# Cross-attention of a decoder layer: weights in chunks, early loads from a second queue, stores moved, products spaced

## What is computed

```python
q = x @ Wq.T ; k_raw = context @ Wk.T ; v_raw = context @ Wv.T
# 32 heads of 16; k and v are read as interleaved pairs of one 1024-wide row
q = rmsnorm(q) ; k = rmsnorm(k)            # over the 16 elements of a head
attn = softmax(q k^T * 16**-0.5)
x = layernorm(x + attn @ v)
```

## Time and profile before

| what | us |
|---|---|
| median of the two timed runs | 2721.75 |
| the profiled execution's own time | 2720.43 |
| its span, first to last instruction | 2718.7 |
| busy: PE | 2443.4 |
| busy: ACT | 1358.8 |
| busy: DVE | 1338.2 |
| busy: POOL | 901.9 |

### The profile page before, as it was taken

One profiled execution on the slowest core, in us unless ns is written; L12 is line 12 of the kernel. 1 busy time (PEld: TensorE's weight loads), 2 busy tenths in 40 slices (PEclk: granted clock), 3 DMA queues, 4 the chain that ended last, 5 costly groups with the idle time before them and its releaser, 6 DMA issues. The chain is left out here.

```text
span 2718.7 us, 38977 instructions
## 1 busy us (share of the span) xinstructions
PE 2443.4 (90%) x15376; PEld 1565.7 (58%) x15376; DVE 1338.2 (49%) x2097; ACT 1358.8 (50%) x1722; POOL 901.9 (33%) x593
## 2 busy tenths in 40 slices
PE   7996799989999999999995899997589999999997
PEld 5875444434444444444224555564478788888776
DVE  5575434334343434343105555554365566666675
ACT  4221357656766777677993443433322255555221
POOL 1234554644465445555003433331022011120320
PEclk9997899999999999999997999999799999999999
DMA  4002665385638554765435100000344266665341
GB/s 170 16 1 80 204 157 137 95 214 146 171 72 227 149 152 102 194 166 140 115 68 200 49 1 16 2 17 1 134 139 131 86 220 211 228 222 176 113 127 51
DMA packets 208437, 333.01 MB, mean 122 GB/s; under 512 B 70976, under 2 KB 125504, under 8 KB 208064
## 3 DMA queue, kind: packets, MB, share of 16 engines
q1 hardware_dynamic: 193200, 262.49, 34.1%
q0 software_dynamic: 15056, 68.03, 7.5%
HBM read 243.10 MB, written 99.42 MB: 126 GB/s over the span
## 5 line engine op out<-in xcount | busy, mean ns | idle before, releaser
L861 ACT ACTIVATE c_prob<-c_psum 128x1024 f32<-128x1024 f32 x832 | 786.3, 1031 | 317.1 <-PE c_psum L1057 308.6
L809 POOL TENSOR_TENSOR c_rr<-c_ms,c_half 128x32 f32<-128x32 f32 (+1 forms) x72 | 372.8, 5179 | 450.0 <-DVE c_ms L878 449.9
L1066 PE MATMUL c_psum<-c_prob,c_vq 128*17 128x512 f32 x3328 | 416.4, 600 | 6.1 <-DVE c_oT L981 6.0
L1057 PE MATMUL c_psum<-c_qq,c_kq 64*128 64x512 f32 x1664 | 292.4, 439 | 35.6 <-ACT c_prob L861 17.7
L1057 PEld LDWEIGHTS c_psum<-c_qq,c_kq 64*128 64x128 f32 x1664 | 137.4, 185 | 196.4 <-ACT c_prob L861 109.7
L918 DVE COPY c_raw<-c_psum 128x256 f32<-128x256 f32 x91 | 38.7, 425 | 364.8 <-PE c_psum L120 364.8
L120 PE MATMUL c_psum<-c_w_hi,c_c_hi 128*128 128x512 f32 x416 | 179.0, 430 | 15.1 <-POOL c_c_lo L802 11.5
L1418 DVE TENSOR_REDUCE s_topx<-s_psum 128x4 f32<-128x2048 f32 (+1 forms) x64 | 95.5, 1492 | 183.3 <-PE s_psum L1508 183.3
L120 PE MATMUL m_psum<-m_t_hi,m_up_hi 128*128 128x256 f32 (+1 forms) x552 | 159.4, 289 | 23.9 <-DVE m_t_lo L2168 23.9
L1941 ACT ACTIVATE m_a_hi<-m_work 128x256 fp32r<-128x256 f32 (+2 forms) x113 | 56.7, 501 | 244.4 <-DVE m_work L2017 238.2
L1066 PEld LDWEIGHTS c_psum<-c_prob,c_vq 128*17 128x17 f32 x3328 | 68.7, 96 | 185.2 <-issue 160.9
(11 more groups left out here) (283 smaller groups left out, 5018.3 us busy)
## 6 DMA issues: line engine op xcount, KB each, us to landing
c_kq<-kd SPq DMA_DIRECT2D x248, 208.0 KB, 6.1
c_c_raw<-in_ctxT SPq DMA_DIRECT2D x104, 256.0 KB, 3.6
c_qq<-qd SPq DMA_DIRECT2D x64, 256.0 KB, 3.2
vd<-c_vt SPq DMA_DIRECT2D x104, 136.0 KB, 2.0
c_vq<-vd SPq DMA_DIRECT2D x31, 442.0 KB, 9.4
kd<-c_t_hi SPq DMA_DIRECT2D x48, 256.0 KB, 2.2
kd<-c_t_lo SPq DMA_DIRECT2D x48, 256.0 KB, 2.6
m_hs<-slots SPq DMA_DIRECT2D x23, 512.0 KB, 7.3
```

Of the source, the lines that this page charges most:

```text
L809: pool.tensor_tensor(rr[:, unit % RB, 0:n], ms[:, unit % RB, 0:n], half[:, 0:n], ALU.pow).then_inc(s_r, 1)
L861: act.activation(prob[:, t % PB, 2 * (u % 2):2 * (u % 2) + 2, :], score_banks[u % 3], ACT.Exp, scale=XD ** -0.5).then_inc(s_ex, 1)
L1057: mm = pe.matmul(score_banks[u % 3][:, s, :], kq[rows, q % 2, u % 2, kt * P:(kt + 1) * P], qq[rows, q % 2, u % 2, :], start=True, stop=True)
L1066: mm = pe.matmul(o_bank[32 * j:32 * j + VW, :], vq[:, q % 2, kt, j, :], prob[:, t % PB, j, :], start=kt == 0, stop=kt == CT - 1)
```

## The change

It is confined to cross-attention:

- Wq is loaded in four chunks with a semaphore each; ACT splits each chunk, DVE makes the low parts after X 0 and X 1 in place of before them, and PE's first query product waits chunk by chunk. The two halves of the key/value weights have a semaphore each.
- KV 13 and KV 14 move from the blocks into the prologue, behind KV 12 (`EARLY = CT + 2`). ACT, not POOL, splits their tiles.
- In the prologue ACT issues the loads of context tiles 4 to 18 itself; from KV 15 on SP loads tile i + 4 ahead of the store of values i.
- Of batch entry 0's queries only chunk 0 is stored in the prologue; chunks 1 to 3 are stored after the load of quad 1. The other entries' stores stay. A quad's load waits for the store of its own chunk alone (`s_qst[c]`).
- The planner wants a block without a heavy piece between a KV and the heavy piece before it, except behind a Q; the due times of a half begin earlier (13 or 10 blocks before its edge in place of 8), even halves end one block earlier, and a heavy piece goes into a block with two value groups after four blocks in place of three.

```diff
+    EARLY = CT + 2
...
-                kv(6), kv(7), t(5), kv(8), kv(9), t(6), kv(10), kv(11), t(7), kv(12)]
+                kv(6), kv(7), t(5), kv(8), kv(9), t(6), kv(10), kv(11), t(7), kv(12), kv(13), kv(14)]
...
+        heavy = [x for x in heavy if x[1:] not in self.of]
...
-            begin, end = (0 if h == 1 else edge(h - 1) - 8), edge(h) - (11 if h % 2 else 13)
+            begin, end = (0 if h == 1 else edge(h - 1) - (13 if h % 2 else 10)), edge(h) - (11 if h % 2 else 14)
...
-        turns = [8, 9, 10]
+        turns = [8, 9, 10, 11]
...
+        unit_done, last_heavy, after_q = {8: -9, 9: -2, 10: -1, 11: -1}, -1, False
...
-                return placed(self.kind_of(self.job_of(kind, i) - 2), 2)
+                return placed(self.kind_of(self.job_of(kind, i) - 2), 2) and last_heavy <= k - 2 + after_q
...
-            elif heavy_ready() and (len(ready) < 2 or k >= due[heavy[0]] + 3):
-                got = heavy.pop(0)
+            elif heavy_ready() and (len(ready) < 2 or k >= due[heavy[0]] + 4):
+                got, last_heavy = heavy.pop(0), k
+                after_q = got[0] == "Q"
...
+        def load_ctx(eng, n):
+            if n >= CB:
+                eng.wait_ge(s_clo, n - CB + 1)
+            eng.dma_start(c_raw[:, n % CB], d["ctxT"][n // CT // 2, n % CT].rearrange("p (k t) -> p k t", k=KC)).then_inc(s_c[n % CB], 16)
...
+                    if piece.i >= line.EARLY and piece.i + CB < 2 * B * CT:
+                        load_ctx(sp, piece.i + CB)
                     store_values(piece)
-                    if piece.i + CB < 2 * B * CT:
-                        load_ctx(piece.i + CB)
-                    if h % 2 == 0 and 4 <= lt < 4 + KC:
+                    if h % 2 == 0 and 4 <= lt < 4 + (KC if h else 1):
                         store_queries(h // 2, lt - 4)
...
-                if g == 0 and first == 0:
-                    sp.wait_ge(s_qst, 16 * 4 * KC * (b + 1))
                 if first == 0:
+                    sp.wait_ge(s_qst[c], 16 * 4 * (b + 1))
...
-            sp.dma_start(wq_raw[:], d["WqT"].rearrange("(k p) n -> p k n", p=P)).then_inc(s_wq, 16)
+            for k in range(KC):
+                sp.dma_start(wq_raw[:, k], d["WqT"][k * P:(k + 1) * P]).then_inc(s_wq[k], 16)
             for i in range(2):
-                load_ctx(i)
+                load_ctx(sp, i)
...
                         load_quad(1, 0, CT, s_quad[1])
+                        for c in range(1, KC):
+                            store_queries(0, c)
...
-                    if job < B * line.JPB and line.kind_of(job)[0] == "KV" and line.kind_of(job)[1] >= CT:
+                    if job < B * line.JPB and line.kind_of(job)[0] == "KV" and line.kind_of(job)[1] >= line.EARLY:
...
-            act.wait_ge(s_wq, 16)
-            act.activation(wq_hi[:], wq_raw[:], ACT.Copy).then_inc(s_whi, 1)
+            for k in range(KC):
+                act.wait_ge(s_wq[k], 16)
+                act.activation(wq_hi[:, k], wq_raw[:, k], ACT.Copy).then_inc(s_wqhi, 1)
...
-            for n in range(CT):
-                if n + 2 < CT:
+            for n in range(line.EARLY):
+                if n + 2 < line.EARLY:
                     high_part(n + 2)
+                load_ctx(act, n + CB)
...
+                if (piece.kind, piece.i) == ("X", 1):
+                    for k in range(KC):
+                        dve.wait_ge(s_wqhi, k + 1)
+                        dve.tensor_tensor(wq_lo[:, k], wq_raw[:, k], wq_hi[:, k], ALU.subtract).then_inc(s_wqlo, 1)
...
+                    if (piece.kind, i) == ("Q", 0):
+                        for k in range(KC):
+                            pe.wait_ge(s_wqlo, k + 1)
+                            mm = product3(pe, dst[:], lambda _: lhs[0](k), lambda _: lhs[1](k), lambda _: rhs[0](k), lambda _: rhs[1](k), 1, first=k == 0, last=k == KC - 1)
+                    else:
+                        mm = product3(pe, dst[:], *lhs, *rhs, KC)
...
```

More of the change, by code:

```diff
@@ L559, in softmax @@
         put_at.update({(p.kind, p.i): -9 for p in self.prologue})
-        unit_done = {8: -9, 9: -2, 10: -1}
+        unit_done, last_heavy, after_q = {8: -9, 9: -2, 10: -1, 11: -1}, -1, False
         done, line_up = 0, self.QT + self.KU
@@ L678, in cross_attention @@
         s_apart = m.sem("apart")
-        s_const, s_w, s_wq, s_whi, s_wlo = m.sem("const", "w", "wq", "whi", "wlo")
+        s_const, s_w, s_wq = m.sem("const"), m.sem("w0", "w1"), m.sem(*[f"wq{k}" for k in range(KC)])
+        s_wqhi, s_wqlo, s_whi, s_wlo = m.sem("wqhi", "wqlo", "whi", "wlo")
         s_c, s_chi, s_clo = m.sem(*[f"c{i}" for i in range(CB)]), m.sem("chi"), m.sem("clo")
@@ L683, in cross_attention @@
         s_ms, s_r, s_kn, s_own = m.sem("ms", "r", "kn", "own")
-        s_qst = m.sem("qst")
+        s_qst = m.sem(*[f"qst{c}" for c in range(KC)])
         s_kst, s_vst, s_quad = m.sem("kst0", "kst1"), m.sem("vst0", "vst1", "vst2"), m.sem("quad0", "quad1")
@@ L717, in store_queries @@
                     for r in range(2):
-                        sp.dma_start(qd[b, c, :, a, :, r, :], part[:, c].bitcast(F32)).then_inc(s_qst, 16)
+                        sp.dma_start(qd[b, c, :, a, :, r, :], part[:, c].bitcast(F32)).then_inc(s_qst[c], 16)
             def store(piece):
@@ L754, in load_quad @@
                 sp.dma_start(vq[:, buf, first:last].rearrange("p l h e -> p l (h e)"), vd[b, :, first:last, g * HG * VW:(g + 1) * HG * VW]).then_inc(s_done, 16)
-            sp.dma_start(wq_raw[:], d["WqT"].rearrange("(k p) n -> p k n", p=P)).then_inc(s_wq, 16)
+            for k in range(KC):
+                sp.dma_start(wq_raw[:, k], d["WqT"][k * P:(k + 1) * P]).then_inc(s_wq[k], 16)
             for i in range(2):
-                load_ctx(i)
+                load_ctx(sp, i)
             for s in range(2):
-                sp.dma_start(w_raw[:, :, s * H:(s + 1) * H], d["WkvT"][:, s * H:(s + 1) * H].rearrange("(k p) n -> p k n", p=P)).then_inc(s_w, 16)
+                sp.dma_start(w_raw[:, :, s * H:(s + 1) * H], d["WkvT"][:, s * H:(s + 1) * H].rearrange("(k p) n -> p k n", p=P)).then_inc(s_w[s], 16)
             for i in range(2, CB):
-                load_ctx(i)
+                load_ctx(sp, i)
             pieces = [(line.FIRST[i], line.FIRST[i + 1]) for i in range(3)]
@@ L768, in first_quad @@
                         if i == 0:
-                            sp.wait_ge(s_wlo, 3)
+                            sp.wait_ge(s_wqlo, KC)
+                            sp.wait_ge(s_wlo, 2)
                         load_quad(0, a, z, s_first[i])
@@ L826, in _ @@
         def _(act):
-            act.wait_ge(s_wq, 16)
-            act.activation(wq_hi[:], wq_raw[:], ACT.Copy).then_inc(s_whi, 1)
+            for k in range(KC):
+                act.wait_ge(s_wq[k], 16)
+                act.activation(wq_hi[:, k], wq_raw[:, k], ACT.Copy).then_inc(s_wqhi, 1)
             def high_weights(s):
-                act.wait_ge(s_w, 32)
+                act.wait_ge(s_w[s], 16)
                 act.activation(w_hi[:, :, s * H:(s + 1) * H], w_raw[:, :, s * H:(s + 1) * H], ACT.Copy).then_inc(s_whi, 1)
@@ L849, in _ @@
                 act.wait_ge(s_put, piece.index + 1)
-                if n % 2 == 0 and unit >= RB:
+                if n % CT % 2 == 0 and unit >= RB:
                     act.wait_ge(s_put, turned_before(unit))
-                act.activation(raw[:, unit % RB, n % 2 * HD:n % 2 * HD + HD], src[:, 0:HD], ACT.Copy).then_inc(s_k, 1)
+                act.activation(raw[:, unit % RB, n % CT % 2 * HD:n % CT % 2 * HD + HD], src[:, 0:HD], ACT.Copy).then_inc(s_k, 1)
                 if v_stored(n):
@@ L891, in low_weights @@
             def low_weights(s):
-                dve.wait_ge(s_whi, s + 2)
+                dve.wait_ge(s_whi, s + 1)
                 dve.tensor_tensor(w_lo[:, :, s * H:(s + 1) * H], w_raw[:, :, s * H:(s + 1) * H], w_hi[:, :, s * H:(s + 1) * H], ALU.subtract).then_inc(s_wlo, 1)
@@ L921, in take @@
                     dve.tensor_copy(vt[:, v_buf(i), :, 0:XD], heads(src[:, HD:H])).then_inc(s_v, 1)
-                if piece.kind == "KV" and early and i + 2 < CT:
+                if piece.kind == "KV" and early and i + 2 < line.EARLY:
                     split_low(i + 2)
@@ L928, in take @@
                         if b and j == 0:
-                            dve.wait_ge(s_qst, 16 * 4 * KC * b)
+                            for c in range(KC):
+                                dve.wait_ge(s_qst[c], 16 * 4 * b)
                         hi, lo = (t[:, :, j * P:(j + 1) * P] for t in (q_hi, q_lo))
@@ L961, in layer_norm @@
                 return LayerNorm(dve, X, lambda t: b * TT + t, (stats, mv, ve, rstd), Count(dve, s_norm, b * LayerNorm.STEPS), s_ve, s_rstd, s_apart, b)
-            dve.wait_ge(s_whi, 1)
-            dve.tensor_tensor(wq_lo[:], wq_raw[:], wq_hi[:], ALU.subtract).then_inc(s_wlo, 1)
             dve.wait_ge(s_const, 4)
@@ L1018, in put @@
                     if piece.kind == "Q":
-                        pe.wait_ge(s_wlo, 1)
```

(5 more changed lines are left out.)

4 lines of the change are left out of this document (removed).

## The result

The changed kernel took 2690.15 us (two runs, 2688.51 to 2691.78) against 2721.75: ratio 0.9884, 95% interval [0.9841, 0.9926]. Run again beside the experiments it took 2687.03 us (ratio 0.9895, [0.9873, 0.9918]). The forecast was 2680, its range 2660 to 2698. The span fell by 31.9 us (2718.7 to 2686.8) where the sum had 41.2.

What follows compares the result with a forecast made beforehand. Prologue bound by what PE waits for, blocks by PE itself. Terms: prologue -20.3, two KV -4.0, spacing -19.5, quad 6 -11.4, stall +14, sum -41.2 us; against 2721.75 this gives 2680 us, range 2660 to 2698.

Steps and rivals of the forecast that it cites:

- Weight, -6.1: Prologue start: chunked loading and splitting let PE's first query product end at 236.6 against 242.7, 6.1 us less.
- Context tiles on ACT: Prologue: tiles issued by ACT remove 15.4 us of PE waits and 4.5 us of half clock behind them.
- rival B: Prologue: tiles late from ACT too, engines being the same 16, and chunks gain only 2.7 us; 2696 us, chance 15%.
- KV 13 and 14 in the prologue, +5.7: Prologue: the two moved products add 12 matmuls each at full clock, 5.7 us together.
- two blocks lose 4.0 us: Blocks that lose KV 13 and KV 14 fall from 4.88 to 2.86 us each, -4.0 us.
- The stall, +14: Block 8: T 12 waits for DVE's copy, held by KV 15's value store behind twelve query stores; 14 us more.
- Rival A: Block 8: the moved stores drain beside quad 1 and hold nobody up; 2666 us, chance 22%.
- Spacing, -19.5: Blocks: spacing heavy pieces ends five PE waits for POOL's split and the half clock after them, -19.5 us.
- Rival D: Blocks: no spacing gain, as another producer, DVE's copies, ends the same waits; 2700 us, chance 8%.
- Quad 6, -11.4: Block 51: an earlier query T piece lets quad 6 load in time; 9.8 us and some 1.6 of half clock go.
- Quads 8, 16 and 24, 0: Blocks near 64 to 69: quad 8's keys are ready later but no loss is taken; 0, bounds 0 and +4 us.
- Rival C: Blocks: SP starves the quads, nine more landing late at 11.4 us each; 2783 us, chance 3%.

Runs made afterwards that it cites:

- single stores: The changed kernel with each query row stored once and read twice by the quad loads, in place of stored twice: 2668.92 us, ratio 0.9821.
- stores in prologue: The changed kernel with all sixteen query stores of the first batch issued in the prologue again, context tiles still on ACT's queue: 2685.55 us, ratio 0.9881.

## Why the prediction was right, step by step

- **Weight, -6.1: size right, reason half right.** Measured -6.5 (16.7 to 10.2). The chunks' loads are 1.4 of it (2.4 at the product's start, 1.0 of which the clock gave back). Four loads landed 2.8 to 5.6 us behind the first issue, the one load 5.6 us behind its own: no loss from the small DMAs. The Trainium skill ("DMA: Bandwidth & Descriptors", "Measured (HBM→SBUF, 128 partitions, SWDGE, issued from GpSimd)") says to batch to 1 MiB, for loads issued from GpSimd; in these, issued from SP, four of 256 KB ended as late as one of 1 MB.
- **"Context tiles on ACT", -19.9: right sum, wrong edit.** The step said that the issue was late and gave the tiles' whole wait to ACT's queue. ACT's queue is worth 4.6 us; 16.6 come from twelve stores that left the stretch. The sum of 21.2 agrees because both parts are in the change. The row that misled was a true one: it names the transfer that was waited for, and not what stood before it. With the stores back, ACT waited 28.1 us for value stores, of which one was issued 9.6 us late and took 7.7 us to land. So lateness of issue, which the step named, is part of it, but it was made by the query stores and held whatever SP issued next. The rule of the Trainium skill cited for rival B ("DMA: Bandwidth & Descriptors", "Issuing engines are not separate DMA queues"), that DMAs of all issuers interleave on the same 16 engines, agrees with the rest: a tile from ACT's queue took 6.9 us beside query stores and 2.6 without. Rival B itself didn't happen: with twelve stores gone, ACT waited 0.5 us for tiles.
- **KV 13 and 14 in the prologue, +5.7.** What is left of the prologue's 19.9 us beside 6.5, 4.6 and 16.6 is +7.8. A wait of 3.4 us behind the value stores came with them; the terms are added as if independent, which wasn't tested. That two blocks lose 4.0 us wasn't measured alone. The prologue as a whole was right to 0.4 us, and that is luck in part: the parts are off by -0.4, -1.3 and +2.1 us, and cancel.
- **The stall, +14: right in chain, the size in part by luck.** Blocks 8 and 9 took 29.0 us against 14.9: +14.1. The chain was shown by three runs, each of which shortened or moved it as the chain says. Inside it the new wait was 16.2 us and not 14, with 2.4 of half clock behind it that the term didn't have. Against that the wait for quad 1 fell from 4.46 to 1.45 us, where the prediction let it stay, and the value matmuls behind it took 1.9 us in place of 3.6, at full clock. Rival A is refuted.
- **Spacing, -19.5: over-counted for the gap.** In the kernel before, the blocks with the five waits (15, 39, 108, 121 and 122, 187) take 19.3 us more than others with the same filling, so the price was right. The five waits went, but two of them also go without the gap, by the two KV that left. The gap alone takes 13 us of waits away, and in this kernel the late quads and block 200 gave all but some 4 us back. Rival D isn't seen: the matmuls of products wait 0.7 us for DVE in all blocks, 1.1 before.
- **Quad 6, -11.4: size about right, cause shared.** Blocks 51 and 52 took 8.0 us in place of 20.7 (0.6 of it because block 52 has no filling now). The wait went with either plan that puts T 21 at most a block behind KV 30; in the kernel before with spread stores alone it stayed (block 51 14.71 us). It landed with no slack: PE still waited 0.3 us.
- **Quads 8, 16 and 24, 0: right, quad 8 by 0.06 us of slack; the missing term was elsewhere.** Quad 7 (block 60, 4.5 us beyond its like; the same block takes 2.73 with single stores) and the value buffer behind quad 23 (blocks 199 to 201, 7.9 us) were costed at nothing. Both shrink where the stores are halved; the second also with a third buffer. Together they are 12.4 us; the blocks gained 9.3 (1098.7 to 1089.4) where the terms for them give 20.9, 11.6 less. The prologue was right to 0.4 us. Rival C had the late quads, but PE waits for quad 7 (3.87 us) and quad 23 (0.6), not for nine.

So the move of the stores, as the change made it, gained nothing: 16.6 us in the prologue, 18.7 lost in blocks 0 to 26 (130.0 against 111.3), and 2685.55 us with it undone against 2687.03. Its gain appears only once they are spread.

## What to carry to other kernels

When an engine waits for a transfer, look at what stands in front of it, in its issuer's order and in bytes on every queue, before crediting a new issuing engine; the next transfer in line can inherit the wait. Work moved off a busy stretch is better moved in portions (here four stores at a time in place of twelve): ask which buffer is freed by the store behind. Remove a stall and a second edit may show its worth only then (the gap: 4 us before, 13 after), so edits are judged again once the queue has room.

## What the runs showed of the hardware

- Four loads of 256 KB, issued 0.4 us apart, ended together with one of 1 MB (5.6 us both), and the first was there after 2.8 us.
- In block 8 PE stood from 339.6 us on; the window from 341.60 to 361.80 shows its granted clock at 0.50 throughout, so T 12 and the start of block 9 ran at 1.2 GHz, and block 9 took 7.28 us in place of 4.88.
- Reading the same rows twice, each time into every other partition, cost less in this kernel than writing them twice: 2668.92 against 2687.03 us.
- Behind query stores SP took 1.90 us to issue a value store, and 0.33 us with none before it (stores in prologue, at 292.62 and 253.71 us).
